# Banded attention: the mask of the maximum's scores moves from a matmul into VectorE's maximum

## The chip, the cores and the metric

The kernel runs on one NeuronCore of a Trainium2 chip. The metric is the time of one execution on the device, in microseconds (us), as the median of several runs. The chip's engines work side by side and wait for each other on semaphores: TensorE (PE in the profile; its weight loads are PEld), VectorE (DVE), ScalarE (ACT), GpSimd (POOL), and SyncE (SP), which here only issues transfers.

## The reference

A transformer of four layers on `x` of 2 x 1024 tokens with 128 channels: full attention, a mixture of experts, banded attention, a mixture of experts, each with a layer norm before it and a residual. What matters here is the banded attention, with 16 heads of width 8:

```python
scores = jnp.einsum('bhid,bhjd->bhij', q, k) * SCALE
valid = (j <= i) & (j >= i - W + 1)          # W = 32
scores = jnp.where(valid, scores, -jnp.inf)
attn = jax.nn.softmax(scores, axis=-1)
out = jnp.einsum('bhij,bhjd->bhid', attn, v)
```

So each query looks at itself and the 31 tokens before it; b and s come from the input, 2 and 1024.

## The kernel before

The banded attention (`attend_banded`) works on NG = 8 groups: 2 batches by 4 groups of 4 heads. A group has 1024 tokens, in 8 tiles of 128. The softmax needs two passes over the scores.

**First pass, for the maximum.** Queries lie on the partitions. For each query tile `qt`, `scores` on TensorE fills two PSUM banks `sc[0]` and `sc[1]`, one for each pair of heads, each 128 x 320: two heads h of BAND = 160 keys (128 of the tile and 32 before it). Each bank first gets a mask (0 inside the band, -1e30 outside) by a matmul of the identity with `mask_q` (L604, 320 columns); then the products of q and k are added onto it, one matmul per head (L609, 160 columns, 48 rows). `reduce_tile` on VectorE takes the negated maximum of each bank in one instruction for both heads (L716). The first tile of a group has no keys before it and uses a mask of its own, `mask_q0`, and 128 columns in L609. The two banks are all there is: the next tile's scores wait until VectorE has read them (`red_done`).

**Between the passes.** After a group's eighth tile, `cut_max` on VectorE splits the maxima into three bf16 parts (four small instructions, L725 to L731), `turn_max` on TensorE transposes them (L632), `copy_max` on ScalarE copies them to SBUF (L684), and `max_rows` on SyncE writes them in six transfers into rows 48 to 50 and 112 to 114 of the queries `qs` (L563).

**Second pass.** Keys lie on the partitions. For each key tile `s`, TensorE fills two banks `st` with a mask (L656) and the products of k with q and its rows of the maximum (L661), ScalarE takes the exponential (L697), and `weigh` on TensorE multiplies by the values (L624).

**Order.** A prologue computes all 8 score tiles of group 0 and the first 4 of group 1. Then stage n is the second pass of group n in 8 steps s; beside it go the score tiles of later groups: steps 0 to 3 hold tiles 4 to 7 of group n+1, steps 4 to 7 hold tiles 0 to 3 of group n+2. TensorE's order in one step is: L656 twice, L661 four times, then the score tile (L604 twice, L609 four times), then `weigh` of the step before. `turn_max(n+1)` stands at the end of step 4. Step 0 of a stage waits for the group's maximum rows (`max_ready`), and step 4 waits for the transfer of group n+2's q and k (`loaded`), since its scores begin there. Stage 6 holds only tiles 4 to 7 of group 7, stage 7 none. SyncE's queue holds, for each stage n, first the 12 transfers of group n+2 (`load_group`, L232; q and k, three sizes), released when the second pass of group n-1 has issued its last product, and then the six of `max_rows(n+1)`. The stages are written as a hardware loop of 2 turns with 3 stages each and two stages behind it.

## Time and profile before

| | us |
|---|---|
| time, median of 3 runs | 1291.75 (1291.39 to 1293.16) |
| the profiled execution's own time | 1291.06 |
| its span in the trace | 1289.2 |
| banded attention in the span, first score matmul to last `weigh` | 817.5 to 957 |
| VectorE busy in the span | 1031.3 (80%) |
| TensorE busy in the span | 1087.0 (84%) |

The span is the time from the first to the last instruction that the profile holds; the time holds 1.9 us more around it. "PE busy" counts a matmul from its start to its modelled end, so waits inside a queue of matmuls count in part as busy. The column PEclk is the clock that TensorE was granted, as a share of 2.4 GHz: 1.00 is 2.4 GHz, 0.50 is 1.2 GHz. In a timeline, a row is a run of like instructions on one engine: start, length, engine, line, what it writes and reads, how many, and in brackets how long the engine was idle before it and for what.

### The profile page before, as it was taken

How to read it: one execution, taken by the hardware profiler on the slowest of the kernel's cores; microseconds unless marked ns; L12 is line 12 of the kernel's file. 1: busy time of each engine (PE TensorE's matmuls, PEld its weight loads, DVE VectorE, ACT ScalarE, POOL GpSimd, SP SyncE). 2: the span in 40 equal slices, each digit the busy share in tenths (PEclk: the TensorE clock that was granted, in tenths of full speed). 3: DMA queues.
4: the chain of work that ended last, by engine and by line, in shares of the span. 5: the costliest groups of instructions: out<-in, count | busy, mean ns of one | idle time of the engine just before them, and what ended most of it. 6: DMA issues, size and time to landing. Idle time of an engine off the chain costs nothing. (4 is left out here: it accounts for less than half of the span.)

```text
span 1289.2 us, 21879 instructions
## 1 busy us (share of the span) xinstructions
PE 1087.0 (84%) x6296; PEld 437.9 (34%) x6296; DVE 1031.3 (80%) x1765; ACT 720.8 (56%) x1103; POOL 400.7 (31%) x316
## 2 busy tenths in 40 slices
PE   4599999899998462999999995598975499999997
PEld 2112222222221051344444443233344244444443
DVE  6798999899999778788888886455537788888886
ACT  3207777677778522566666666045543356666665
POOL 1000000000000302676777770000001267777675
PEclk9658999899999776999999998589986699999999
DMA  2800000000002810767776651312100177766663
GB/s 66 249 4 26 26 27 1 27 26 21 6 2 93 278 32 3 162 161 166 161 162 158 155 117 47 102 52 58 45 2 20 44 177 165 159 156 155 162 161 95
DMA packets 53388, 120.14 MB, mean 93 GB/s; under 512 B 10296, under 2 KB 36792, under 8 KB 45128
## 3 DMA queue, kind: packets, MB, share of 16 engines
q1 hardware_dynamic: 53320, 119.28, 37.2%
q8 instruction: 37, 0.61, 0.2%
q14 instruction: 31, 0.25, 0.1%
HBM read 103.94 MB, written 14.91 MB: 92 GB/s over the span
## 5 line engine op out<-in xcount | busy, mean ns | idle before, releaser
L476 DVE TENSOR_REDUCE Aatt_mx<-Aatt_sc 128x1 f32<-128x512 f32 x512 | 317.4, 683 | 25.5 <-PE Aatt_sc L352 25.0
L436 ACT ACTIVATE Aatt_prob<-Aatt_st 128x1024 f32<-128x1024 f32 x256 | 247.3, 1022 | 76.5 <-PE Aatt_st L361 75.0
L1392 POOL TENSOR_TENSOR M1ex_low<-M1ex_hid,M1ex_high 128x512 f16<-128x512 f32 x132 | 180.8, 1387 | 95.0 <-ACT M1ex_high L1324 92.1
L1392 POOL TENSOR_TENSOR M2ex_low<-M2ex_hid,M2ex_high 128x512 f16<-128x512 f32 x132 | 179.6, 1378 | 94.5 <-ACT M2ex_high L1324 93.2
L352 PE MATMUL Aatt_sc<-ks,qs 48*128 48x512 bf16 x512 | 176.9, 432 | 27.3 <-DVE Aatt_mx L476 5.8
L372 PE MATMUL Aatt_pv<-Aatt_prob,vg 128*32 128x512 f32 x1024 | 143.4, 633 | 0.8 <-ACT Aatt_prob L436 0.6
L1363 DVE TENSOR_TENSOR M1ex_hid<-M1ex_act_up,M1ex_cb 128x512 f32<-128x512 f32 x132 | 138.4, 1049 | 4.9 <-DMA M1ex_cb<-comb 4.9
L1363 DVE TENSOR_TENSOR M2ex_hid<-M2ex_act_up,M2ex_cb 128x512 f32<-128x512 f32 x132 | 139.0, 1053 | 4.0 <-DMA M2ex_cb<-comb 4.0
L1354 DVE SCALAR_TENSOR_TENSOR M1ex_act_up<-M1ex_up,unscale,M1ex_sil 128x512 f32<-128x512 f32 x132 | 98.4, 746 | 37.0 <-ACT M1ex_sil L1319 34.6
L1319 ACT ACTIVATE M1ex_sil<-M1ex_gate,unscale 128x512 f32<-128x512 f32 x132 | 90.7, 687 | 64.9 <-PE M1ex_gate L1272 61.1
L1354 DVE SCALAR_TENSOR_TENSOR M2ex_act_up<-M2ex_up,unscale,M2ex_sil 128x512 f32<-128x512 f32 x132 | 98.4, 746 | 35.4 <-ACT M2ex_sil L1319 31.2
L1319 ACT ACTIVATE M2ex_sil<-M2ex_gate,unscale 128x512 f32<-128x512 f32 x132 | 90.7, 687 | 61.7 <-PE M2ex_gate L1272 57.9
L352 PEld LDWEIGHTS Aatt_sc<-ks,qs 48*128 48x128 bf16 x512 | 38.4, 95 | 227.1 <-DVE Aatt_mx L476 208.6
L326 POOL COPY vg<-A_vn 128x256 f32 (+1 forms) x8 | 3.2, 402 | 353.3 <-PE Aatt_pv L372 311.9
L361 PE MATMUL Aatt_st<-qs,ks 51*128 51x512 bf16 x512 | 102.2, 400 | 6.2 <-ACT Aatt_prob L436 3.6
L716 DVE TENSOR_REDUCE Batt_m<-Batt_sc 128x2 f32<-128x320 f32 x128 | 57.0, 488 | 60.8 <-PE Batt_sc L609 60.6
L1324 ACT CAST M2ex_high<-M2ex_hid 128x512 f16<-128x512 f32 x132 | 80.9, 613 | 34.1 <-DVE M2ex_hid L1363 32.0
L1324 ACT CAST M1ex_high<-M1ex_hid 128x512 f16<-128x512 f32 x132 | 80.9, 613 | 33.6 <-DVE M1ex_hid L1363 33.0
L697 ACT ACTIVATE Batt_prob<-Batt_st 128x320 f32<-128x320 f32 x128 | 49.0, 435 | 55.5 <-PE Batt_st L661 55.4
L1270 PE MATMUL M1ex_gate<-M_xh,M_wt 128*128 128x512 f16 x132 | 50.7, 384 | 27.1 <-DVEq L1348 23.9
L1270 PE MATMUL M2ex_gate<-M_xh,M_wt 128*128 128x512 f16 x132 | 50.5, 383 | 26.3 <-DVEq L1348 23.9
L1282 PE MATMUL M1ex_acc<-M1ex_low,M_wt 128*128 128x512 f16 x132 | 50.3, 381 | 2.0 <-POOL M1ex_low L1392 2.0
(271 smaller groups left out, 1774.8 us busy)
## 6 DMA issues: line engine op xcount, KB each, us to landing
M1ex_cb<-comb SPq DMA_DIRECT2D x64, 512.0 KB, 6.5
M2ex_cb<-comb SPq DMA_DIRECT2D x64, 512.0 KB, 6.5
M_wt<-wsplit SPq DMA_DIRECT2D x66, 192.0 KB
wsplit<-split_cut SPq DMA_DIRECT2D x9, 704.0 KB, 7.0
split_raw<-in_wg_dram SPq DMA_DIRECT2D x6, 704.0 KB, 5.1
stack<-Aqkv_part SPq DMA_DIRECT2D x16, 192.0 KB, 3.2
qs<-stack SPq DMA_DIRECT2D x32, 96.0 KB
ks<-stack SPq DMA_DIRECT2D x32, 96.0 KB
```

Of the source, the lines that this page charges most:

```text
L352: pe.matmul(sc_bank(k, i)[:, :], qs[k][rows, jp, qt * P:(qt + 1) * P], ks[k][rows, jp, h * CH:(h + 1) * CH], start=True, stop=True).then_i ...
L361: mm = pe.matmul(st[jp][:, half, :], ks[k][rows, jp, kc * P:(kc + 1) * P], qs[k][rows, jp, qh * CH:(qh + 1) * CH], start=True, stop=True)
L372: mm = pe.matmul(pv[32 * j:32 * j + 32, :], vg[k][:, kc, j, :], prob[(2 * s + j % PAIR) % 4][:, j // PAIR, :], start=kc == 0, stop=kc == T ...
L436: act.activation(prob[e % 4][:, :, :].rearrange("p a c -> p (a c)"), st[pr][:, :, :].rearrange("p a c -> p (a c)"), ACT.Exp, scale=SCALE). ...
L476: dve.tensor_reduce(mx[k][:, m, part // 2:part // 2 + 1], sc_bank(k, i)[:, :], AX.X, ALU.max).then_inc(red_done, 1)
L716: dve.tensor_reduce(m1[k][:, 2 * pr:2 * pr + 2, qt], sc[pr][:, :].rearrange("p (h r) -> p h r", h=2), AX.X, ALU.max, negate=True).then_inc ...
L1270: pe.matmul(o, wt[k][:, a, :], env.xh[:, cs], start=True, stop=False)
L1319: act.activation(sil[i % 2][:, :], gate[i % 2][:, :], ACT.Silu, scale=env.unscale[:, 0:1]).then_inc(sil_ready, 1)
L1324: act.copy(high[i % 3][:, :], hid[i % 3][:, :]).then_inc(high_ready, 1)
L1354: dve.scalar_tensor_tensor(act_up[i % 3][:, :], up[i % 2][:, :], env.unscale[:, 1:2], sil[i % 2][:, :], ALU.mult, ALU.mult).then_inc(up_re ...
L1363: dve.tensor_tensor(hid[i % 3][:, :], act_up[i % 3][:, :], cb[k][:, c * CH:(c + 1) * CH], ALU.mult).then_inc(hid_ready, 1)
L1392: pool.tensor_tensor(low[i % 3][:, :], hid[i % 3][:, :], high[i % 3][:, :], ALU.subtract).then_inc(low_ready, 1)
```

## The change

The mask matmuls of the first pass go. TensorE writes the products alone, each with `start=True`; for each head VectorE then runs one `tensor_tensor_reduce`, which adds the mask from SBUF to the scores in PSUM, negates, writes the result back over the scores and gives the minimum into `m1`. That is four instructions of 160 (first tile 128) elements for a tile instead of two of 320. The third mask goes, with its five GpSimd instructions in the set-up. In the same edit the hardware loop of the banded stages is replaced by eight stages written out, so that no wait counts on a register.

```diff
-        LOOPED = 6
-        def stages(eng, stage):
-            with eng.Fori(0, LOOPED // 3) as i:
-                for k in range(3):
-                    stage(i, k, True, True)
-            stage(LOOPED // 3, 0, True, False)
-            stage(LOOPED // 3, 1, False, False)
+        def stages(stage):
+            for n in range(NG):
+                stage(n // 3, n % 3, n + 1 < NG, n + 2 < NG)
...
             def scores(n, k, qt):
-                mask = mask_q if qt else mask_q0
-                for pr in range(2):
-                    pe.wait_ge(red_done, n * 2 * STEPS + 2 * qt + pr + 1)
-                    pe.matmul(sc[pr][:, :], env.ident16[:, :], mask[:, :], start=True, stop=True)
                 first = 0 if qt else WIN
                 for h in range(2):
                     for pr in range(2):
+                        if h == 0:
+                            pe.wait_ge(red_done, n * 2 * STEPS + 2 * qt + pr + 1)
                         rows = slice(HALF * pr, HALF * pr + MAXROW)
                         mm = pe.matmul(sc[pr][:, h * BAND + first:(h + 1) * BAND], qs[k][rows, h, qt * P:(qt + 1) * P],
-                                       ks[k][rows, h, qt * P - WIN + first:(qt + 1) * P], start=False, stop=True,
-                                       skip_group_check=True)
+                                       ks[k][rows, h, qt * P - WIN + first:(qt + 1) * P], start=True, stop=True)
                         if h == 1:
                             mm.then_inc(sc_done, 1)
...
             def reduce_tile(n, k, qt):
+                first = 0 if qt else WIN
                 for pr in range(2):
                     dve.wait_ge(sc_done, n * 2 * STEPS + 2 * qt + pr + 1)
-                    dve.tensor_reduce(m1[k][:, 2 * pr:2 * pr + 2, qt], sc[pr][:, :].rearrange("p (h r) -> p h r", h=2),
-                                      AX.X, ALU.max, negate=True).then_inc(red_done, 1)
+                    for h in range(2):
+                        j = 2 * pr + h
+                        scores = sc[pr][:, h * BAND + first:(h + 1) * BAND]
+                        ins = dve.tensor_tensor_reduce(scores, scores, mask_q[:, first:BAND], -1.0, -BARRED, ALU.add, ALU.min,
+                                                       accum_out=m1[k][:, j, qt:qt + 1])
+                    ins.then_inc(red_done, 1)
```

## Rows read from the trace of the kernel before

**Rows 1.** Groups of instructions, 812 to 950 us: count, busy us, mean ns, idle before.

```profile
L716 DVE TENSOR_REDUCE Batt_m<-Batt_sc 128x2 f32<-128x320 f32 x128 | 57.0, 488 | 60.8 <-PE Batt_sc L609 60.6
```

**Rows 2.** Windows: length, busy of each engine, PEclk, DMA share, GB/s.

```profile
817.00:839.00 22.00, 13.82 (x69) 3.99 (x69) 10.54 (x26) 1.54 (x2) 0.80 (x2) 0.50 0.21 58
839.60:849.90 10.30, 10.30 (x75) 2.72 (x74) 4.17 (x10) 3.06 (x8) 0.00 (x0) 0.50 0.25 73
850.00:957.80 107.80, 96.70 (x1207) 38.22 (x1206) 47.89 (x125) 56.89 (x144) 2.41 (x6) 0.97 0.14 39
...
943.00:946.00 3.00, 0.93 (x7) 0.32 (x7) 0.00 (x0) 0.48 (x2) 0.00 (x0) 0.96 0.00 0
```

**Rows 3.** Timeline of the prologue, last tile of group 0, and its maximum.

```profile
830.72 0.45 PE L609 MATMUL Batt_sc<-ks,qs 48*128 48x160 bf16 x4
831.20 0.89 DVE L716 TENSOR_REDUCE Batt_m<-Batt_sc 128x2 f32<-128x320 f32 x2 [0.92 <-PE Batt_sc L609]
...
834.08 3.74 SPq L563 DMA_DIRECT2D qs<-Batt_mt  x6
```

**Rows 4.** Timeline of stage 3, steps 1 and 2.

```profile
889.90 0.31 PE L609 MATMUL Batt_sc<-ks,qs 48*128 48x160 bf16 x4
...
890.25 0.89 DVE L716 TENSOR_REDUCE Batt_m<-Batt_sc 128x2 f32<-128x320 f32 x2 [0.65 <-PE Batt_sc L609]
...
890.55 0.45 PE L656 MATMUL Batt_st<-mask,ident 128*128 128x320 bf16 x2
...
891.18 0.45 PE L604 MATMUL Batt_sc<-mask,ident 128*128 128x320 bf16 x2
...
891.55 0.31 PE L609 MATMUL Batt_sc<-ks,qs 48*128 48x160 bf16 x4
...
891.80 0.48 PE L624 MATMUL Batt_pv<-Batt_prob,vg 128*32 128x160 f32 x8
```

**Rows 5.** Timeline of TensorE: steps of stages 0, 1, 3 and 4, one transpose.

```profile
839.60 0.71 PE L656 MATMUL Batt_st<-mask,ident 128*128 128x320 bf16 x2
...
849.89 0.56 PE L656 MATMUL Batt_st<-mask,ident 128*128 128x320 bf16 x2
...
864.41 0.45 PE L656 MATMUL Batt_st<-mask,ident 128*128 128x320 bf16 x2 [0.18 <-DMA ks<-stack]
...
887.37 0.44 PE L656 MATMUL Batt_st<-mask,ident 128*128 128x320 bf16 x2 [1.19 <-DMA qs<-Batt_mt]
...
893.86 0.45 PE L656 MATMUL Batt_st<-mask,ident 128*128 128x320 bf16 x2
895.50 0.26 PE L632 MATMUL Batt_turn<-ident,Batt_mparts 128*96 128x128 bf16 x1
...
901.53 0.44 PE L656 MATMUL Batt_st<-mask,ident 128*128 128x320 bf16 x2 [0.70 <-DMA qs<-Batt_mt]
```

**Rows 6.** Timeline of SyncE's queue: issues of maximum rows (L563) and loads (L232).

```profile
852.71 3.68 SPq L563 DMA_DIRECT2D qs<-Batt_mt  x6
...
862.01 0.74 SPq L232 DMA_DIRECT2D ks<-stack  x2
...
896.56 3.68 SPq L563 DMA_DIRECT2D qs<-Batt_mt  x6
900.62 0.81 SPq L232 DMA_DIRECT2D qs<-stack  x2
...
905.22 0.74 SPq L232 DMA_DIRECT2D ks<-stack  x2
...
924.83 17.32 SPq L563 DMA_DIRECT2D qs<-Batt_mt  x12
```

**Rows 7.** Groups of VectorE instructions, whole span, as Rows 1.

```profile
L820 DVE TENSOR_TENSOR Bout_att<-Bout_ut,Bout_rden 128x128 f32<-128x128 f32 x16 | 4.7, 292 | 0.6
...
L210 DVE TENSOR_TENSOR B_vn<-Bqkv_pv,b_bv 128x512 f32<-128x512 f32 x4 | 2.7, 688 | 2.6 <-PE Bqkv_pv L155 2.6
...
L92 DVE BATCH_NORM_AGGREGATE Aqkvln_mv<-Aqkvln_stats 128x2 f32<-128x6 f32 x16 | 1.2, 152 | 0.0
```

More of the change, by code:

```diff
@@ L536, in attend_banded @@
         block = ctx.enter_context(nc.Block())
-        mask_q, mask_q0, mask_k = env.masks
-        LOOPED = 6
-        def stages(eng, stage):
-            with eng.Fori(0, LOOPED // 3) as i:
-                for k in range(3):
-                    stage(i, k, True, True)
-            stage(LOOPED // 3, 0, True, False)
-            stage(LOOPED // 3, 1, False, False)
+        mask_q, mask_k = env.masks
+        def stages(stage):
+            for n in range(NG):
+                stage(n // 3, n % 3, n + 1 < NG, n + 2 < NG)
         def score_blocks(s, k, nxt, nxt2):
@@ L577, in stage @@
                     max_rows(n + 1, (k + 1) % 3)
-            stages(sp, stage)
+            stages(stage)
         @block.gpsimd
@@ L594, in stage @@
                     copy_v(n + 1, (k + 1) % 3)
-            stages(pool, stage)
+            stages(stage)
         @block.tensor
@@ L672, in stage @@
                 weigh(n, k, STEPS - 1)
-            stages(pe, stage)
+            stages(stage)
         @block.scalar
@@ L705, in stage @@
                         copy_max(n + 1)
-            stages(act, stage)
+            stages(stage)
         @block.vector
@@ L745, in stage @@
                             cut_max(n + off, kk)
-            stages(dve, stage)
+            stages(stage)
 def project_out(nc, env, tag):
@@ L881, in _ @@
                                    pattern=[[-1, P]], channel_multiplier=1).then_inc(made, 1)
-            pool.wait_ge(made, 7)
+            pool.wait_ge(made, 6)
             def keep(m, base, step, multiplier):
@@ L888, in keep @@
                                    pattern=[[0, 2], [step, BAND]], channel_multiplier=multiplier).then_inc(made, 1)
-            mq, mq0, mk = env.masks
-            for m in (mq, mq0):
-                keep(m, -1, 1, -1)
+            mq, mk = env.masks
+            keep(mq, -1, 1, -1)
             keep(mk, 0, 1, -1)
+            pool.wait_ge(made, 8)
+            keep(mq, WIN, -1, 1)
+            keep(mk, WIN - 1, -1, 1)
             pool.wait_ge(made, 10)
-            for m in (mq, mq0):
-                keep(m, WIN, -1, 1)
-            keep(mk, WIN - 1, -1, 1)
-            pool.wait_ge(made, 13)
-            keep(mq0, -WIN, 1, 0)
-            pool.wait_ge(made, 14)
             for m in (env.fresh, env.fresh_groups):
                 pool.memset(m[:, :, :], 1.0).then_inc(made, 1)
-            pool.wait_ge(made, 16)
+            pool.wait_ge(made, 12)
             for m in (env.fresh, env.fresh_groups):
                 pool.memset(m[:, :, 0:1], 0.0).then_inc(made, 1)
-            pool.wait_ge(made, 18)
+            pool.wait_ge(made, 14)
 def attention(nc, env, a, tag, attend):
@@ L1419, in transformer @@
         env.ident16 = sb("ident16", [P, P], BF16)
-        env.masks = [sb(f"mask{i}", [P, 2 * BAND], BF16) for i in range(3)]
+        env.masks = [sb(f"mask{i}", [P, 2 * BAND], BF16) for i in range(2)]
         env.gate = sb("gate_w", [P, E], F32)
```

## The prediction

> **What bounds the kernel now.** I read the page first, then the stretch of the banded attention by windows, groups, timeline and waits, since everything that changes in the run is there (817.5 to 957 us of the span). The groups say who waits: VectorE's 128 reductions are busy for 57.0 us, and VectorE is idle for 60.8 us before them, for the score matmuls [rows 1]. The windows say that there are three regimes [rows 2]: the prologue, with TensorE at half clock (1.2 GHz) and busy for 63%; the first 10 us of stage 0, still at half clock but without a gap; and the rest, at 2.4 GHz for nearly all of it.
>
> *Prologue.* TensorE and VectorE take turns on two banks. A tile takes 0.92 + 0.89 = 1.81 us: VectorE reduces for 0.89 us and waits 0.92 us, of which 0.48 us lie between the first product's start and the reduction's, and 0.44 us before that, which is the hand-over and the second mask matmul [rows 3].
>
> *Stages.* From one step's score products to the next's are 891.55 - 889.90 = 1.65 us: second pass 0.63, score mask 0.37, score products 0.25, `weigh` the remaining 0.40 [rows 4]. That looks as if 0.37 us of each step could be had. The timeline of the stages says otherwise. A stage begins when the maximum rows have landed; TensorE was idle for 1.19 and 0.70 us before that [rows 5]. From the transpose at the end of step 4 to the next stage's start there are 901.53 - 895.50 = 6.03 us: 1.06 us to the first issue (896.56), 3.68 us of issuing, the landing, and the start 4.97 us after the first issue [rows 5, 6]. Steps 5 to 7 lie under this chain; a shorter step there only lengthens TensorE's wait. What counts is the way from a stage's start to its transpose, 895.50 - 887.37 = 8.13 us. Before its last step lies a second chain, on SyncE: loads begin 4.06 us after the first maximum issue, take 905.96 - 900.62 = 5.34 us to issue, and step 4 may not begin before they land. In stage 1, where step 4 did wait for them, it began at 864.41, 1.66 us after the last issue ended at 862.75 [rows 5, 6]. So step 4 can't begin sooner than 6.1 us after the stage's start (4.06 + 5.34 + 1.66 - 4.97), and it begins 893.86 - 887.37 = 6.49 us after it now [rows 5, 6]. The clean stage-to-stage time is 8.13 + 6.03 = 14.16 us; the mean over five stages, from first maximum issue to first maximum issue, is (924.83 - 852.71) / 5 = 14.42 us, with the other stages' waits for loads and slower issues in it [rows 6].
>
> **The change, part by part.** *TensorE* loses the two mask matmuls of each of 64 tiles: 0.37 us a step at 2.4 GHz [rows 4], and at half clock between 0.53 us (640 columns) and 0.74 us (twice 0.37); I take 0.64. A step is then 1.28 us of TensorE's own work. At half clock the first four steps take 849.89 - 839.60 = 10.3 us, the first without `weigh` (about 0.7): 2.75 us a step, 2.1 after the change [rows 5].
>
> *VectorE* gets four passes for two. Call D its time from a tile's first to its last. The new operation is not in the trace. A two-input pass over PSUM takes 292 ns for 128 elements and 688 ns for 512 [rows 7], so 1.03 ns an element and 160 ns fixed: 325 ns for 160. Passes without a wait overlap: two reductions of 488 ns end after 0.89, so the second starts 0.40 after the first, some 0.09 before its end [rows 1, 4], and sixteen small instructions of 152 ns are busy for 1.2 us together, 0.075 us each [rows 7]. So a pass costs 165 + 75 = 0.24 us, and the last one 0.325. Lower bound: D = 3 x 0.24 + 0.325 = 1.05 us. Upper bound: each pass in full, with a small instruction for the minimum, and no overlap: 4 x (0.325 + 0.075) = 1.60 us. With the overlap and the small instruction it is 4 x 0.075 more than the lower one, 1.35. I take the middle, 1.30, against 0.89 now. The first tile has 128 elements, 0.13 less.
>
> The Trainium skill (VectorE: DVE Perf Modes, "Two Vector instructions with no wait between them") says that an operation that also writes out its accumulator is two instructions, the main one and a read of the accumulator. No row here shows it. By it the sum goes with 1.35, about 1.6 us later than mine; the same page's "Rules for kernel authors" asks for fewer instructions, which speaks against the change.
>
> *The turn between the two.* TensorE can now run the first product of bank 0 while VectorE still reads bank 1. After VectorE's last pass there follow 0.05 us of hand-over and the second and third product. The first three took 0.35 us to the reduction's start at 2.4 GHz (889.90 to 890.25) and 0.48 us at half clock [rows 3, 4]. I take 0.34 and 0.44 us from the end of one tile's passes to the start of the next's, where 0.65 and 0.92 stand now. A tile in a stage then takes D + 0.34 = 1.64 us, more than TensorE's 1.28: VectorE becomes the bound, and the 0.37 us is eaten. In the prologue: D + 0.44 = 1.74 against 1.81.
>
> *The sum.*
> - Prologue, group 0: seven turns of 0.07 less, 0.13 for the short first tile and 0.6 because its products start without the masks, against 0.4 because the last tile's passes take 1.30 for 0.89: -0.8 us.
> - Start of stage 0: now 839.60, 5.52 us after the maximum's first issue at 834.08, behind group 1's four tiles [rows 3, 5]. The rows land about 5 us after the first issue: -0.3 us.
> - Stage 0 to the next maximum's issue, 852.71 - 839.60 = 13.1 us [rows 5, 6]: five masks less at half clock are -3.2, but the last step, which ran at full clock (the clock rose at 850, rows 2), comes before the rise: +1.0, so 10.9. VectorE's chain gives 11.3: second pass at half clock 1.26 and turn 0.44, three steps of 2.1, D, and 834.08 - 832.09 = 1.99 from the last reduction's end to the issue [rows 3]. I take -1.8.
> - Five stages: from a stage's start, VectorE's first pass comes at 0.63 + 0.34 = 0.97; three tiles of D + 0.34; D; `cut_max` and hand-over 1.99 - 1.06 = 0.93: 2.92 + 4 D = 8.12 against 8.13. With 6.03 behind it 14.15 us: no gain over a clean stage. Of the 5 x (14.42 - 14.15) = 1.35 us of irregular waits I take -0.9, because TensorE reaches step 4 earlier in its work and SyncE and ScalarE lose the loop's turn. That covers the written-out loop too: its ends cost little since they lie under the maximum's transfers, and the longer instruction stream I price at 0, with up to 1 us either way.
> - Stage 6 to the last maximum: +0.1. Stage 7 has no scores. The set-up loses five GpSimd instructions; SyncE's loads end it, so 0.
>
> Together -0.8 - 0.3 - 1.8 - 0.9 + 0.1 = -3.7 us. The profiled execution's own 1291.06 us (span 1289.2 and 1.9 around it) becomes 1287.3. The median of the runs is 0.7 above that execution, so 1288.0 us.
>
> **Rivals.** D stands on this path 8 + 1 + 5 x 4 + 4 = 33 times, so 0.1 us of D is 3.3 us.
> 1. *The new passes are cheap* (D = 1.05): the prologue and stages 0 and 6 gain 13 x 0.25 = 3.2 more; the five stages stop at the loads: 6.1 + 0.63 + 0.25 + 0.41 = 7.4 to the transpose, a stage of 13.4, so 5 x 0.75 = 3.8 more. 1288.0 - 7.0 = 1281.0. For it: two-input passes run at one element a cycle. Against it: something has to write the minimum out.
> 2. *The new passes are dear and VectorE holds the stages up* (D = 1.60): +9.9 on -3.7, so 1297.9 us. It decides from D = 1.41, where the sum is zero. For it: every instruction here has 160 ns of its own, and twice as many are issued on the chain that decides; the scores are also written back. Against it: the overlap seen between reductions.
> 3. *It cancels* (D between 1.33 and 1.49): within 2.6 us of 1291.8. For it: the two maskings cost nearly the same, and the second chain is untouched.
> 4. *The clock stays low.* The granted clock was 1.2 GHz while TensorE was 63% busy, rose after 10 us at 100%, and fell to 1.2 GHz at 946 after a window at 31% [rows 2]. After the change TensorE's own work is 1.28 of 1.64 us in a step, and the full-height mask matmuls are half as many. If it never rises, a stage is 1.7 + 3 x 2.1 + 1.3 + 0.93 = 10.2 us to the transpose and three steps and a `weigh` behind it, 7.0: 17.2 us, so 5 x 2.8 and about 2.4 in the last stages on the first -2.9, about 1305. For it: less activity. Against it: at half clock TensorE has 2.1 us of work against VectorE's 1.74, no gap, and it is idle at every stage's start already. The Trainium skill (TensorE: Matmul & The Clock Gate, "What's actually happening") says that activity is what releases the clock; the windows agree.
>
> **Chances.** Forecast, D from 1.15 to 1.33 (1283 to 1289): 0.36. Rival 1: 0.16. Rival 3: 0.20. Rival 2: 0.20. Rival 4: 0.08. From no change a measurement here can tell about 0.2%, 2.6 us. Faster: 0.36 + 0.16 = 0.52; within: 0.20; slower: 0.28. The range reaches from rival 1's end to past D = 1.60: 1281 to 1299 us; the forecast's own is 1283 to 1289.
>
> **What the profile after would show.** L604 gone; the new VectorE row at 320 to 400 ns, four of them in 1.05 to 1.60 us, gaps of 0.34 us between tiles in the stages; a tile of about 1.74 us in the prologue; stages 14.2 us apart, waiting for VectorE before the transpose; TensorE's idle time up; the clock at 1.00 from about 850. It is wrong if D is over 1.41, if the clock falls inside the stages, or if the maximum rows or loads land at other times.

## The result and the profile after

| | before | after |
|---|---|---|
| median of 4 runs, us | 1292.05 (1291.39 to 1293.16) | 1278.21 (1273.47 to 1282.75) |
| the profiled execution's own time | 1291.06 | 1279.5 |
| its span | 1289.2 | 1277.7 |
| banded attention in the span, first score matmul to last `weigh` | 817.48 to 956.91 = 139.43 | 820.42 to 949.77 = 129.35 |
| VectorE busy | 1031.3 | 1051.1 |
| TensorE busy | 1087.0 | 1064.8 |

The ratio is 0.9893, with a 95% interval from 0.9864 to 0.9922: faster by 1.1%. The forecast was 1288.0 with a range from 1281 to 1299, so the time is below the range. The direction was right, the size was not: 3.7 us forecast, 13.8 measured (the prediction's 3.7 starts from 1291.75, the median of three runs). The set-up lost four GpSimd instructions and not five: one fill of the third mask and three that cut it to the band. In the profiled executions 10.1 us of the difference of 11.5 in span lie in the banded attention. Of the kernel before, two runs further down, 1303.34 and 1381.65 us, had a lower granted clock over the whole run (0.889 and 0.789 for about 0.90) and are left out of the ratios.

The groups of instructions from 812 to 945 us of the kernel after, to be read beside [rows 1]:

```profile
L712 DVE CUSTOM_DVE_ANT_0 Batt_sc<-Batt_sc,mask 128x160 f32<-128x160 f32 x224 | 66.1, 357 | 26.7 <-PE Batt_sc L602 26.7
...
L712 DVE DVE_READ_ACCUMULATOR2_ANT Batt_m<- 128x1 f32 x256 | 36.2, 141 | 0.0
...
L712 DVE CUSTOM_DVE_ANT_0 Batt_sc<-Batt_sc,mask 128x128 f32<-128x128 f32 x32 | 8.3, 322 | 6.0 <-PE Batt_sc L602 6.0
```

Each new pass is two rows, the pass of 357 ns and a read of the accumulator of 141 ns. VectorE is now idle for 26.7 + 6.0 us before its passes, where it was idle for 60.8 us. How long a tile really takes is in the timeline of the prologue, one tile and the start of the next, to be read beside [rows 3]:

```profile
822.35 0.33 DVE L712 CUSTOM_DVE_ANT_0 Batt_sc<-Batt_sc,mask 128x160 f32<-128x160 f32 x1 [0.41 <-PE Batt_sc L602]
822.60 0.14 DVE L712 DVE_READ_ACCUMULATOR2_ANT Batt_m<- 128x1 f32 x1
822.60 0.36 DVE L712 CUSTOM_DVE_ANT_0 Batt_sc<-Batt_sc,mask 128x160 f32<-128x160 f32 x1
822.88 0.14 DVE L712 DVE_READ_ACCUMULATOR2_ANT Batt_m<- 128x1 f32 x1
822.88 0.36 DVE L712 CUSTOM_DVE_ANT_0 Batt_sc<-Batt_sc,mask 128x160 f32<-128x160 f32 x1
823.07 0.10 PEld L602 LDWEIGHTS Batt_sc<-ks,qs 48*128 48x128 bf16 x1 [0.96 <-DVE Batt_m L712]
...
823.44 0.14 DVE L712 DVE_READ_ACCUMULATOR2_ANT Batt_m<- 128x1 f32 x1
...
823.99 0.33 DVE L712 CUSTOM_DVE_ANT_0 Batt_sc<-Batt_sc,mask 128x160 f32<-128x160 f32 x1 [0.41 <-PE Batt_sc L602]
```

The read of one pass and the next pass start together, and passes start 0.25 us (behind the first) to 0.28 us apart. From the first start to the end of the last read it is 823.58 - 822.35 = 1.23 us: that is D, forecast 1.30. The turn to the next tile is 0.41 us, forecast 0.44. At 823.07 TensorE loads for bank 0 while VectorE is still in bank 1, as foreseen.

The timeline around a transpose of the stages, from the kernel after, and the starts of stages 3 and 4. They answer to [rows 5, 6]:

```profile
861.17 0.33 DVE L712 CUSTOM_DVE_ANT_0 Batt_sc<-Batt_sc,mask 128x160 f32<-128x160 f32 x1 [0.34 <-PE Batt_sc L602]
...
863.26 0.59 ACT L694 COPY B_u<-Batt_pv 128x512 f32<-128x512 f32 x1
...
863.35 0.26 PE L624 MATMUL Batt_turn<-ident,Batt_mparts 128*96 128x128 bf16 x1 [0.18 <-DVE Batt_mparts L728]
...
863.73 0.29 ACT L676 COPY Batt_mt<-Batt_turn 96x128 bf16<-96x128 bf16 x1
...
864.10 3.67 SPq L558 DMA_DIRECT2D qs<-Batt_mt  x6
...
868.97 0.45 PE L648 MATMUL Batt_st<-mask,ident 128*128 128x320 bf16 x2 [0.38 <-DMA qs<-Batt_mt]
...
882.35 0.45 PE L648 MATMUL Batt_st<-mask,ident 128*128 128x320 bf16 x2 [0.34 <-DMA qs<-Batt_mt]
...
891.05 4.44 SPq L558 DMA_DIRECT2D qs<-Batt_mt  x6
...
896.72 0.72 PE L648 MATMUL Batt_st<-mask,ident 128*128 128x320 bf16 x2 [1.35 <-DMA qs<-Batt_mt]
```

The transpose now waits for VectorE, 0.18 us, where it had no wait in stage 3 before. The turn is 0.34 us. From the transpose to the first maximum issue are 864.10 - 863.35 = 0.75 us, where it was 1.06; the copy of the maximum, L676, is ready to run almost as soon as the transpose ends. A clean stage is 882.35 - 868.97 = 13.38 us, forecast 14.15. The last three rows show one that is not clean: the maximum's issues took 4.44 us for 3.67, TensorE waited 1.35 us, and its first two mask matmuls then took 0.72 us for 0.45.

The windows of the kernel after show the clock behind the last of these (length, busy of each engine, PEclk, DMA share, GB/s), to be read beside [rows 2]:

```profile
820.50:840.00 19.50, 8.52 (x49) 2.63 (x48) 14.14 (x93) 1.54 (x2) 0.28 (x1) 0.50 0.19 52
840.50:850.00 9.50, 9.29 (x93) 3.65 (x93) 6.70 (x45) 3.86 (x11) 0.00 (x0) 0.56 0.31 84
850.00:949.00 99.00, 82.71 (x1076) 34.53 (x1074) 62.22 (x406) 54.23 (x140) 2.40 (x6) 0.95 0.16 43
...
893.00:896.00 3.00, 2.17 (x35) 0.82 (x34) 2.47 (x16) 1.67 (x5) 0.40 (x1) 1.00 0.05 10
896.00:899.00 3.00, 2.28 (x17) 1.00 (x17) 0.88 (x7) 0.79 (x3) 0.00 (x0) 0.59 0.58 169
899.00:902.00 3.00, 2.89 (x30) 1.05 (x29) 1.72 (x13) 1.10 (x4) 0.00 (x0) 0.50 0.41 97
```

TensorE's granted clock fell to 1.2 GHz at 896.6, at the end of the 1.35 us wait, and rose at 903.4. It fell once more, from 940.9 to 944.3, behind the 1.38 us wait before stage 7.

Why stage 4 began late shows in the traffic. Besides the kernel's own transfers, the queues carry the kernel's instructions in packets of 16 KB. The views show packets, MB and share for each queue: first the kernel after over the late passage (893 to 897), then over 879 to 930, and last the kernel before over 879 to 930.

```profile
q8 instruction: 1, 0.02, 2.0%
```

```profile
q8 instruction: 4, 0.07, 0.5%
```

```profile
q1 hardware_dynamic: 1776, 2.46, 17.3%
q14 instruction: 2, 0.02, 0.1%
```

The one packet of the late passage started at 893.85, while maximum rows were under way. The transfer issued at 893.50 landed 2.96 us later, where 1.74 is usual, and the issue behind it took 1.35 us for 0.59. The 14 traces kept here hold 98 passages from a stage's transpose to the next stage. From the first maximum issue to the last landing, 69 of them take 4.82 to 5.05 us and 29 take 5.16 to 6.43. In 28 of the 29 a 16 KB instruction packet starts in between, and in one of the 69. That the packet delays the transfers is read from this coincidence; no run moved a packet on purpose. Over the second turn of the hardware loop the kernel before has no such packet (none between 878.7 and 930.9; those of q14 are of 8 KB), the kernel after has four.

The 10.1 us, step by step, worked out from the timelines of both:

| stretch | before | after | gain | forecast |
|---|---|---|---|---|
| first score matmul to first transpose | 15.55 | 14.01 | 1.5 | 0.8 |
| that transpose to stage 0 | 6.57 | 5.99 | 0.6 | 0.3 |
| stage 0 | 18.07 | 15.15 | 2.9 | 1.8 |
| stages 1 to 5 | 72.04 | 69.69 | 2.4 | 0.9 |
| stage 6 | 15.08 | 13.53 | 1.6 | -0.1 |
| stage 7 | 12.12 | 10.98 | 1.1 | 0 |

The forecast's terms end at the maximum's issues and not at the stages' starts, so they stand beside the nearest stretch. In the table below "to transpose" is from a stage's start to its transpose, and "behind" from there to the next start.

| stage, after | 0 | 1 | 2 | 3 | 4 | 5 | 6 |
|---|---|---|---|---|---|---|---|
| to transpose | 9.32 | 7.78 | 7.78 | 7.77 | 9.17 | 7.77 | 7.78 |
| behind | 5.83 | 5.62 | 5.60 | 6.60 | 6.00 | 5.60 | 5.75 |

### The profile page after: what moved, and what is told of

The parts are those of the page before. It is cut to its first block and busy times, and to the rows that moved or that the text cites. A ratio compares the mean times of both kernels' runs of the same rounds, so it can differ in the third digit from the quotient of the medians.

```text
span 1277.7 us, 21430 instructions
## 1 busy us (share of the span) xinstructions
PE 1064.8 (83%) x6168; PEld 435.2 (34%) x6168; DVE 1051.1 (82%) x2149; ACT 719.0 (56%) x1102; POOL 401.5 (31%) x312
## 5 line engine op out<-in xcount | busy, mean ns | idle before, releaser
L712 DVE CUSTOM_DVE_ANT_0 Batt_sc<-Batt_sc,mask 128x160 f32<-128x160 f32 (+1 forms) x256 | 74.4, 353 | 32.8 <-PE Batt_sc L602 32.8
L602 PE MATMUL Batt_sc<-ks,qs 48*128 48x160 bf16 (+1 forms) x256 | 34.4, 259 | 21.9 <-DVE Batt_m L712 16.1
```

The lines of the kernel that those rows point to most:

```text
L712: ins = dve.tensor_tensor_reduce(scores, scores, mask_q[:, first:BAND], -1.0, -BARRED, ALU.add, ALU.min, accum_out=m1[k][:, j, qt:qt + 1])
```

## Experiments

Three sets of kernels were run, each set on one chip beside the kernel before. In the first set that kernel took 1293.60 us (median of 23 runs), in the second 1293.05 (11), in the third 1291.85 (7). Its runs were spread further than the four above: 1282.38 to 1303.34 in the first set. The ratios are to the kernel before of the same set, and differ a little from the quotient of the medians. The banded part is that of the one profiled execution of each kernel.

| kernel | median us | ratio (95%) | banded part |
|---|---|---|---|
| the kernel after again | 1278.65 | 0.9874 (0.9828 to 0.9921) | 129.56 |
| stages written out only | 1287.21 | 0.9961 (0.9929 to 0.9993) | 136.85 |
| mask in VectorE, loop kept | 1282.79 | 0.9915 (0.9883 to 0.9948) | 129.53 |
| no mask at all | 1277.47 | 0.9898 (0.9842 to 0.9953) | 129.97 |
| VectorE's half alone | 1298.26 | 1.0048 (1.0024 to 1.0073) | 150.72 |
| after, one more pass a tile | 1284.08 | 0.9924 (0.9906 to 0.9941) | 140.03 |
| written out, maximum's copy first | 1282.11 | 0.9911 (0.9877 to 0.9945) | 134.34 |
| after, bank by bank | 1277.40 | 0.9890 (0.9866 to 0.9915) | 130.01 |
| after, filler at stage starts | 1274.46 | 0.9857 (0.9814 to 0.9899) | 129.33 |
| bank by bank, both fillers | 1272.70 | 0.9856 (0.9816 to 0.9896) | 125.30 |
| bank by bank, filler in steps | 1277.75 | 0.9897 (0.9857 to 0.9938) | 130.02 |
| no mask, filler in steps | 1277.31 | 0.9874 (0.9817 to 0.9931) | 129.17 |

### The kernel after again, and the change in two parts

The kernel after was run once more, unchanged.

> The changed kernel again, as the others' neighbour on the same chip, and because its four runs spread over 9 us where the kernel before spreads over 2. Theory A with the clock: the time again 1274 to 1283, the low ones with TensorE's clock at 1.00 in all of stages 1 to 6, the high ones with a stretch at 0.50 in them, as from 896 to 904 us in the first profile. Rival: the spread was chance of four runs, all within 2 us now.

It took 1278.65 us, and its clean stages are again 7.78 and 5.60. It too has one slow passage behind stage 3's transpose (6.45) and then the clock at half from 893 to 900, stage 4 with 9.23 to the transpose. Both profiled executions of the kernel have it. The spread of the first four runs was not an accident of four: six more lie between 1273.91 and 1281.41. Whether the short ones keep the clock through all stages, as expected, is not shown, since the profiled execution was the longest.

The next kernel is the one before with the stages written out, and nothing else:

```diff
-        def stages(eng, stage):
-            with eng.Fori(0, LOOPED // 3) as i:
...
+        def stages(stage):
+            for n in range(NG):
+                stage(n // 3, n % 3, n + 1 < NG, n + 2 < NG)
```

> The kernel before with only the loop of the banded stages written out; masks stay on TensorE. Theory A (the gain is the mask's move: shorter way from a stage's start to the transpose, and a shorter prologue): between 0 and -1.5 us against 1292.0, stages still 14.1 to 14.2 us apart, 8.1 us from a stage's start to its transpose. Rival B (the written-out stages give a good part of the 13.8 us, by fewer register instructions, branches and table loads): -4 us or more.

Its median is 0.4% below that of the kernel before, about 5 us (0.9 to 9.2), where 0 to 1.5 had been expected: by the time alone the rival, 4 us or more, is not excluded. In the traces it has 2.6 us less in the banded part. Its clean stages are 8.13 to the transpose and 5.86 behind it, where before had 8.13 and 5.94 to 6.04: 0.08 to 0.18 us of each stage was the loop's. But stages 1 to 5 together take 72.06 us for 72.04, since two slow passages (6.68 and 6.74) took it back. The 2.6 us lie elsewhere: 0.3 in stage 0, 1.2 in stage 6, where the part behind fell from 7.06 to 5.86, and 1.15 in stage 7, from 12.12 to 10.97. In the kernel before a 16 KB instruction packet started at 942.69, under the last maximum transfer, which landed after 3.19 us for 1.75; TensorE waited 2.70 us, and the clock was low from 945.7 to 952.6. The written-out kernel waited 1.49 us and had it low from 948.0 to 951.4. So these 2.4 us are where a packet fell, and not clearly the loop's.

The other half: the mask in VectorE, with the hardware loop left on TensorE, ScalarE, GpSimd and SyncE, and VectorE alone written out. The loop on VectorE with the new passes was not tried.

```diff
-            stages(stage)
+            stages(stage, pe)      # on sp, pool and act in the same way
...
+            with eng.Fori(0, LOOPED // 3) as i:
+                for k in range(3):
+                    stage(i, k, True, True)
```

> The mask in VectorE as in the changed kernel, but with the loop kept on TensorE, ScalarE, GpSimd and SyncE (VectorE's part written out). Theory A: within 2 us of the changed kernel's 1278.2, so -11 to -14; stages 13.4 us apart, 7.8 us from start to transpose. Rival B: it loses 4 us or more of the gain, so 1282 or later.

Its banded part is 129.53 us, that of the kernel after. Clean stages are 7.78 and 5.70. So in the traces the mask's move carries the gain, and the written-out stages add at most 0.1 us a stage to it; the two parts do not add up. By the time it is less clear: the median, 1282.79, is 4.1 us above that of the kernel after in the same set and so on the side of the rival (1282 or later), but the two intervals overlap, and the profiled execution (1277.05) is one of its shorter ones.

### What VectorE's time does to the stages

VectorE's half of the change alone, on the kernel with the stages written out: TensorE still writes its masks, and VectorE adds the mask once more.

```diff
-                    dve.tensor_reduce(m1[k][:, 2 * pr:2 * pr + 2, qt], sc[pr][:, :].rearrange("p (h r) -> p h r", h=2),
-                                      AX.X, ALU.max, negate=True).then_inc(red_done, 1)
+                    for h in range(2):
...
+                        ins = dve.tensor_tensor_reduce(scores, scores, mask_q[:, first:BAND], -1.0, -BARRED, ALU.add, ALU.min,
+                                                       accum_out=m1[k][:, j, qt:qt + 1])
```

> VectorE's half alone: its four passes for a tile as in the changed kernel, but TensorE's mask matmuls stay (so the mask is added twice, which leaves the result as it is). Written-out stages. Theory A (a tile is VectorE's time D plus the turn to TensorE and back; both halves of the change act on this sum): D stays 1.23, the turn stays 0.65 us in the stages and 0.92 in the prologue; a prologue tile 2.15 us, start to transpose 1.34 + 3 x 1.88 + 1.23 + 0.93 = 9.1 us, stages 14.8 us apart, banded part about 5 us longer than the 136.9 of the run with only the stages written out. Rival (VectorE's extra time hides behind TensorE's): 136 to 138, start to transpose 8.1.

The timeline of its stage 3 shows two tiles:

```profile
909.62 0.33 DVE L715 CUSTOM_DVE_ANT_0 Batt_sc<-Batt_sc,mask 128x160 f32<-128x160 f32 x1 [0.65 <-PE Batt_sc L604]
...
910.72 0.14 DVE L715 DVE_READ_ACCUMULATOR2_ANT Batt_m<- 128x1 f32 x1
...
911.51 0.33 DVE L715 CUSTOM_DVE_ANT_0 Batt_sc<-Batt_sc,mask 128x160 f32<-128x160 f32 x1 [0.65 <-PE Batt_sc L604]
```

The turn is 0.65 us, as in [rows 4], and D is 910.86 - 909.62 = 1.24. A tile is 1.89 us, 0.24 more than the 1.65 of before, where TensorE still set the step. To the transpose there are three such tiles and the last D, which is 0.35 longer than 0.89: 8.13 + 3 x 0.24 + 0.35 = 9.20 us. Measured are 9.17 to 9.18 in five of seven stages. VectorE's passes set the transpose. The banded part missed its forecast, though: 13.9 us more than with the stages written out alone, where about 5 had been expected. The prologue took 2.6 us more, and stage 2 took 18.21 us with the clock low from 881 to 891.

Then the kernel after with one more pass a tile, a reduction of 160 elements of the mask that nobody reads:

```diff
                     dve.wait_ge(sc_done, n * 2 * STEPS + 2 * qt + pr + 1)
+                    if pr == 1:
+                        dve.tensor_reduce(extra[:, 0:1], mask_q[:, 0:BAND], AX.X, ALU.max)
```

> The changed kernel with one idle VectorE pass more in each tile (a reduction of 160 elements of the mask into a scratch column), which raises D by about 0.24 us. Theory A: D stands on the path about 33 times, so start to transpose 7.78 + 4 x 0.24 = 8.7 us, a prologue tile 1.89, the banded part 129.4 + 33 x 0.24 = 137 us. Rival (the loads or the maximum's transfers set the stages at 13.4, and VectorE only follows): start to transpose under 8.2, the banded part 129 to 132.

```profile
L711 DVE TENSOR_REDUCE Batt_extra<-mask 128x1 f32<-128x160 bf16 x58 | 18.2, 314 | 0.0
```

The groups from 830 to 950 show the pass with 314 ns. The transpose came after 8.85 us in stages 3, 5 and 6, 1.07 more than 7.78, so four tiles of 0.27. The banded part rose by 10.7 us, where the added passes make 33 x 0.27 = 8.9: besides them the clock was low at 865 to 871, 902 to 909, 919 to 923 and 940 to 953. The profiled execution, 1291.24 us, is the longest of the five, 7 us above their median.

Now the other way. This kernel leaves the first pass's mask out altogether, as its expectation says: two plain reductions of the raw scores a tile.

```diff
-                        ins = dve.tensor_tensor_reduce(scores, scores, mask_q[:, first:BAND], -1.0, -BARRED, ALU.add, ALU.min,
-                                                       accum_out=m1[k][:, j, qt:qt + 1])
...
+                    dve.tensor_reduce(m1[k][:, 2 * pr:2 * pr + 2, qt], sc[pr][:, :].rearrange("p (h r) -> p h r", h=2)[:, :, first:BAND],
+                                      AX.X, ALU.max, negate=True).then_inc(red_done, 1)
```

> Leaves work out: the maximum is taken over the unmasked scores, one reduction per bank, and no engine adds the mask there. It gives the price of the mask in VectorE. Theory A: VectorE's time for a tile falls from 1.23 to 0.89 us; the prologue's tile from 1.65 to about 1.30, so 3 us less with the start of stage 0; the stages can't fall under the 13.4 us which the loads of the group after next allow, so they gain 0 to 0.3 each: 1273 to 1275. Rival C (VectorE's chain still sets the stages): start to transpose 1.4 us shorter, stages 12.0 us apart, 1265. Rival D (the mask in VectorE is hidden): same as the changed kernel.

VectorE had its 0.89 us back and TensorE no masks to write, and the time was that of the kernel after, not the 1273 to 1275 us expected. The timeline from the first transpose that comes early, 6.68 us after its stage's start:

```profile
868.38 0.45 PE L648 MATMUL Batt_st<-mask,ident 128*128 128x320 bf16 x2 [0.54 <-DMA ks<-stack]
869.53 0.12 PEld L624 LDWEIGHTS Batt_turn<-ident,Batt_mparts 128*96 128x96 bf16 x1
...
869.82 0.59 ACT L694 COPY B_u<-Batt_pv 128x512 f32<-128x512 f32 x1
870.28 0.28 ACT L676 COPY Batt_mt<-Batt_turn 96x128 bf16<-96x128 bf16 x1
870.65 3.67 SPq L558 DMA_DIRECT2D qs<-Batt_mt  x6
...
874.44 1.85 SPq L232 DMA_DIRECT2D qs<-stack  x2
...
877.13 0.71 PE L648 MATMUL Batt_st<-mask,ident 128*128 128x320 bf16 x2 [3.04 <-DMA qs<-Batt_mt]
```

Step 4 waited 0.54 us for the loads: the second chain binds. The maximum's copy stands behind the 0.59 us copy of `B_u` again and the first issue is 1.12 us after the transpose. Then TensorE had nothing to do for 3.04 us, and the two mask matmuls behind that took 0.71 us. Of the 3.04 us, 1.6 are a late landing: an instruction packet started at 874.72, and the last maximum transfer, issued at 873.74, took 3.35 us. Before stages 1, 2, 4, 5 and 6 the wait was 0.9 to 2.0 us, where the kernel after has 0.34 to 0.75 in all stages but two. The windows of the same kernel:

```profile
875.00:878.00 3.00, 0.87 (x6) 0.36 (x8) 0.00 (x0) 0.00 (x0) 0.00 (x0) 0.66 0.29 102
878.00:881.00 3.00, 3.00 (x28) 1.09 (x24) 1.78 (x4) 1.53 (x4) 0.00 (x0) 0.50 0.60 159
881.00:884.00 3.00, 3.00 (x31) 1.32 (x34) 0.97 (x3) 1.06 (x3) 0.00 (x0) 0.50 0.01 3
```

The clock was at 1.2 GHz from 876.0 to 886.2, and the next stage needed 9.24 us to its transpose. What was won on VectorE's chain came back as waiting at a stage's end, and the low clock took it away.

### The copy of the maximum

Before with the stages written out, and ScalarE's copy of the turned maximum put ahead of its copy of `B_u`:

```diff
+                    if s == STEPS - AHEAD + TURN and nxt:
+                        copy_max(n + 1)
                     if s in (TB // 2, STEPS - 1):
...
-                    if s == STEPS - AHEAD + TURN and nxt:
-                        copy_max(n + 1)
```

> Masks on TensorE, stages written out, and ScalarE copies the turned maximum before it copies the first half of the output, where the kernel before has them the other way round. Theory S (part of the gain is that, with the transpose later than the last product, this copy no longer waits behind the other): from the transpose to the first issue 0.75 us for 1.06, transpose to next stage 5.55 instead of 5.86, so 7 x 0.3 = 2 us less in the banded part (136.9 to about 134.8). Rival: the copy's order costs nothing, 5.86 stays.

The timeline of ScalarE and SyncE, first in the kernel with the stages written out, then in this one:

```profile
883.00 0.26 PE L627 MATMUL Batt_turn<-ident,Batt_mparts 128*96 128x128 bf16 x1
883.14 0.58 ACT L697 COPY B_u<-Batt_pv 128x512 f32<-128x512 f32 x1 [0.23 <-PE Batt_pv L619]
883.62 0.27 ACT L679 COPY Batt_mt<-Batt_turn 96x128 bf16<-96x128 bf16 x1
...
883.98 3.67 SPq L558 DMA_DIRECT2D qs<-Batt_mt  x6
```

```profile
877.68 0.26 PE L627 MATMUL Batt_turn<-ident,Batt_mparts 128*96 128x128 bf16 x1
877.98 0.26 ACT L679 COPY Batt_mt<-Batt_turn 96x128 bf16<-96x128 bf16 x1 [0.38 <-PE Batt_turn L627]
878.14 0.58 ACT L699 COPY B_u<-Batt_pv 128x512 f32<-128x512 f32 x1
878.33 3.67 SPq L558 DMA_DIRECT2D qs<-Batt_mt  x6
```

The issue comes 0.65 us after the transpose and not 0.98; the part behind is 5.52 for 5.86 while the part to the transpose stays 8.13; and the banded part is 2.5 us shorter. The kernel after gets nearly the whole of this without the edit: there VectorE delays the transpose past the `weigh` that ends step 4, the copy of `B_u` starts before the transpose (863.26 against 863.35), and the copy of the maximum no longer waits for it.

### The order of the products, and the clock

The kernel after with the products of bank 0 first and then those of bank 1, so that the turn gets shorter:

```diff
-                for h in range(2):
-                    for pr in range(2):
+                for pr in range(2):
+                    for h in range(2):
```

> The changed kernel, but TensorE issues both products of bank 0 and then both of bank 1, so that bank 0 is full again while VectorE is still on bank 1. Theory A: the turn goes (0.34 us in the stages, 0.41 in the prologue): a prologue tile 1.2 to 1.3 us, start to transpose under 7.4 where the loads stop it, so 3 us less before stage 0 and 0.3 a stage, if the clock holds. Rival H (the clock falls, as without any mask, because TensorE does too little): stretches at 0.50 in half the stages, start to transpose 8 us and more there, no gain in the stages; banded part 127 to 130.

The prologue went from 14.01 to 11.00 us, and one stage ran at full clock with 7.01 and 5.74, 12.75 us. The other stages took 14.2 to 15.2, each with a stretch at low clock. The windows over its stage 3:

```profile
875.00:878.00 3.00, 2.52 (x29) 1.17 (x30) 2.05 (x15) 1.53 (x4) 0.00 (x0) 0.99 0.35 105
878.00:881.00 3.00, 3.00 (x28) 1.13 (x27) 1.54 (x11) 0.77 (x2) 0.00 (x0) 0.50 0.51 149
881.00:884.00 3.00, 2.83 (x38) 1.32 (x34) 2.55 (x17) 1.49 (x4) 0.00 (x0) 0.50 0.03 8
```

If the waits cost the clock and the clock the gain, then matmuls without use, put into the waits, should win it back. Four kernels put some there. All write a bank that the next real mask overwrites: "filler at starts" stands before a stage's wait for its maximum rows, "filler in steps" beside the second pass's mask. The first has four at each start:

```diff
+                if n:
+                    pe.wait_ge(exp_done, n * 2 * STEPS + 1)
+                    for _ in range(4):
+                        pe.matmul(st[k][:, :], env.ident16[:, :], mask_k[:, :], start=True, stop=True)
                 pe.wait_ge(max_ready, MAX_IN * n + MAX_IN)
```

> The changed kernel with four matmuls of the second pass's mask (320 columns each, into the bank that step 0 overwrites) before TensorE waits for a group's maximum rows, stages 1 to 7. They give nothing but work in the wait. Theory H (the clock falls in stage 3 or 4 because of the idle time before a stage, longest where the maximum's transfers are slow): no stretch at 0.50 between 850 and 935 us, stages 3 and 4 at 13.4 and 14.4 us for 14.4 and 15.2, banded part 129.5 to about 127.5. Rival (the stretch comes from the lower activity inside the steps): it stays, 129 to 130.

The banded part, 129.33, didn't move: a slow passage of 7.40 us behind stage 2's transpose still came before a low clock, at 881 to 884, and took about 1.8 us more than a clean one. What came back was 1.1 us in stage 7, 9.87 for 10.98, and 1.4 in stage 4, whose way to the transpose was 7.78 for 9.17.

The second has bank by bank, six at the starts and one more mask matmul in each step:

```diff
-                        pe.matmul(bank[:, :], env.ident16[:, :], mask_k[:, :], start=True, stop=True)
+                        for _ in range(2 - pr if n else 1):
+                            pe.matmul(bank[:, :], env.ident16[:, :], mask_k[:, :], start=True, stop=True)
```

> Products bank by bank, with six such matmuls before each stage's wait and one more in every step of stages 1 to 7 (TensorE's own work 1.41 us a step). Theory H: clock at 1.00 in stages 1 to 6, start to transpose 7.3 us, stages 12.9 to 13.2; with the prologue's 4 us less than the changed kernel's the banded part 121 to 124 us, the time 1270 to 1273. Rival (falls of the clock have another cause than TensorE's activity): as bank by bank alone, stages at 14 to 15 us and 130.

```profile
846.00:939.00 93.00, 85.49 (x1114) 40.84 (x1114) 57.22 (x376) 50.54 (x131) 2.00 (x5) 1.00 0.17 46
```

In its windows the clock is 1.00 from 846 to 939. The banded part is 125.30 us, a little over the 121 to 124 expected and the shortest of all, though the fillers lengthened the way to the transpose to 7.42, and though two passages behind a transpose were slow (6.92 and 7.07 us). At 1272.70 us (1271.71 to 1274.87) it has the lowest median here, but its ratio is that of the filler at stage starts, and its interval overlaps with most others. It differs from bank by bank alone, at 130.01, only in work that is of no use, and is 4.7 us shorter in the banded part, with one execution of each in the profile: that is what the held clock brought here, less the fillers' own time.

The third has bank by bank and two more mask matmuls a step, none at the starts:

```diff
+                        for _ in range(2 if n else 1):
+                            pe.matmul(bank[:, :], env.ident16[:, :], mask_k[:, :], start=True, stop=True)
```

> Products bank by bank, with two such matmuls more in every step of stages 1 to 7 and none in the waits: the mask matmuls' columns are those of the kernel before, but they stand in no exchange with VectorE (TensorE's own work about 1.55 us a step). Theory H: clock at 1.00, start to transpose 7.6 to 7.9, stages 13.3 to 13.6, banded part 124 to 126. Rival: 130 as without them.

Its banded part is 130.02, a miss: the way to the transpose was 7.83 to 7.88 where the clock was full, but the clock was low at 845 to 848 and 917 to 920, and two passages took 6.86 and 7.27. (The profiled execution, 1272.36 us, is the shortest of its four.)

The fourth leaves the first pass's mask out again and has two more mask matmuls of the second pass a step:

> Leaves work out: the maximum over unmasked scores, as in the run without any mask, with two such matmuls more in every step of stages 1 to 7. Theory H (that run was held back by the clock, in five of seven stages, not by the loads alone): start to transpose 7.4 to 7.6 instead of 8.5, stages 13.2 to 13.5 instead of 14.2 to 15.8, banded part 124 to 126 instead of 130. Rival (the run without the mask was bound by loads and transfers): about 130 again.

The banded part was 129.17, again a miss. One stage took 13.04 us, with 7.15 to the transpose; five others took 14.2 to 14.9, with the clock still low in three stretches and step 4 waiting up to 1.21 us for the loads.

## Why the prediction was wrong in size

**The bound, right.** The way from a stage's start to its transpose and from there over ScalarE, SyncE and the landing is what sets the stages, not TensorE's 1.65 us a step. [rows 5, 6] said so. The two kernels with more VectorE time moved with it; the one with less did so only in the one stage whose way was at full clock (6.68 us), where the loads bound it.

**D, mis-sized.** It is 1.23 and not 1.30. The prediction took the middle between an estimate with the accumulator's read (1.35) and a bound without it (1.05). There is a read, and it costs no time of its own on this chain but the last: it starts with the next pass. The Trainium skill (VectorE: DVE Perf Modes, "Two Vector instructions with no wait between them") says that such an operation is two instructions; the rows of 357 and 141 ns agree, and adding the second in full would have been wrong here. A pitch of 0.25 to 0.28 us carried the sum: 2.92 + 4 x 1.23 = 7.84 us to the transpose, measured 7.78, forecast 8.12. By the prediction's own count of 33 places this term is 33 x 0.07 = 2.3 us.

**"With 6.03 behind it", the step that failed.** The prediction took the part behind the transpose as unchanged. It is 5.60 us in clean stages. Of the 0.43, the kernels apart show 0.08 to 0.18 for the written-out stages, which were priced at nothing, and the rest for the copy of the maximum, which no longer stands behind the copy of `B_u` on ScalarE. The prediction had followed TensorE's and SyncE's queues past the transpose, but not ScalarE's, and the copy put first by hand shortened the banded part by 2.5 us, of which 7 x 0.34 us at most are the copy's own.

Both together make a clean stage 7.78 + 5.60 = 13.38 for 14.15, and five of them 3.9 us. Not all of it arrived: stages 1 to 5 gained 2.4 us. The slow passage before stage 4 cost 1.0 us, the low clock behind it 1.4 in stage 4's way to the transpose, and a second slow passage, behind that transpose at full clock, 0.4; on the other side 1.2 us of such irregular waits in the kernel before went. An instruction packet starts in each of the two slow passages, at 893.85 and 907.50. So the longer instruction stream, which the prediction priced at 0 with up to 1 us either way, is a second term of the prediction that the traces contradict: it brings packets into stages where the loop had none, and one of them, with the clock behind it, stands for 2.4 us.

**Stage 0 and prologue, mis-sized.** Tiles of the prologue are 1.65 us apart, forecast 1.74: seven turns make the 0.6 us that are missing, 0.5 of it D's. In stage 0 the first maximum issue came 850.69 - 840.42 = 10.27 us after the start, forecast 11.3. VectorE's first pass came at 1.39 and not 1.70; three steps took 847.56 - 841.81 = 5.75 and not 6.3, since the first interval holds no `weigh`, which the prediction had noted for TensorE's steps and not for VectorE's chain; and 1.90 followed D for 1.99.

**Stages 6 and 7.** 1.6 and 1.1 us came where nothing was forecast. The kernel with only the stages written out has nearly both (1.2 and 1.15). They are mostly not the change's: 1.3 us of them are the late landing of one transfer before stage 7 in the kernel before, under an instruction packet, and 1.1 the clock, which is low for 6.9 us of stage 7 before (945.7 to 952.6) and for 3.4 after (940.9 to 944.3). With one profile of the kernel before, it is not shown how often that happens to it.

**The remainder.** 13.8 us in the medians against 10.1 in the banded part. Of the profiled executions 1.4 us lie outside it. The stretch from the output projection to the second mixture takes 55 us in some executions and 58 to 60 in others, in kernels whose code there is the same: 55.2 after, 58.2 before, 60.0 with the stages written out alone. The two profiled executions of the kernel after alone have 55.2 and 60.0, so the edit does not set it. The interval of the ratio, 10.1 to 17.6 us, is for the whole time of one set of four runs each. The traces account for 10.1 us, 2.4 of them the packet and the clock of stages 6 and 7; what the rest of the 13.8 is, they don't show. Nor do the two mis-sized terms reach the measured time by themselves: 2.3 us for D and 5 x 0.43 = 2.2 for the part behind turn 1288.0 into 1283.5.

**The rivals.** Rivals 2 and 3 needed D above 1.33 and are out. Rival 1 had the right sign of the error and the wrong cause: D isn't 1.05 but 1.23, about a quarter of the way from 1.30, and its time came close by the copy and by irregular waits. Its floor was wrong as well: without any mask, step 4 waited for the loads at 868.38, 5.5 us after its stage's start (862.85), not 6.1; the loads began 3.8 us behind the first maximum issue for 4.06 and took 4.84 us to issue for 5.34. What it missed most is that a still cheaper VectorE brings nothing more: without any mask the banded part is 129.97 us. Rival 4 came true in part: the clock does rise, at 848.8, but it falls again in stages 4 and 7, which the prediction had named as a sign of being wrong, and costs 1.4 us in the first and 1.1 in the second (10.98 us, where two kernels with the same stage and the clock at 1.00 take 9.87) rather than 17. The Trainium skill (TensorE: Matmul & The Clock Gate, "What's actually happening") ties the clock to activity; the kernel with both fillers agrees, with 1.00 in place of 0.82 over 846 to 939 and 4.7 us less.

What sets the fall is more than the wait. The kernel with only the stages written out also waited 1.35 us, before its stage 5, and kept 1.00; so did bank by bank with filler in the steps after 1.42 us. Both have more mask matmuls in their steps than the kernel after, whose clock fell behind 1.35 us in both profiled executions. But bank by bank with filler in the steps also lost it, behind 1.02 and 1.84 us, and no mask with filler in the steps behind 1.25 to 1.51. So the runs show that more work on TensorE can hold the clock, and no rule for when it is enough.

**What stays open.** In nearly every kernel one or two passages behind a transpose are slow (5.9 to 7.6 us for 5.6), with maximum issues of 4.0 to 5.0 us for 3.67 or, where the last transfer is the late one, a landing of 2.7 to 3.4 us. Instruction packets start in 28 of the 29; that they are the cause no run separated, and the traces don't say which engine's instructions they hold. Nor is it settled why two more matmuls a step held the clock less well than one, with six at the starts: no run varied the one at a fixed number of the other.

## What to carry to other kernels

Behind a stage's bound, follow the result through every engine's queue down to the next stage's start: a copy of 0.59 us on an engine that was only half busy stood on the path in six of seven stages. Where the end of that path is a row of small transfers, look for instruction packets among them before pricing a longer program at nothing. Price an unseen pass by the pitch between its starts, not by the sum of its rows. And when a chain is shortened whose end is a fixed wait of TensorE, look at the granted clock behind that wait: past a point the next microsecond won there is paid back (no mask at all, 129.97 us), and cheap matmuls can then win more than the work saved (both fillers, 125.30).

## What the runs showed of the hardware that was not expected

- A `tensor_tensor_reduce` with an accumulator over 160 elements in PSUM is a row of 357 ns and one of 141 ns, at a pitch of 0.28 us (0.25 behind a tile's first); over 128 elements it is 0.25 us (0.21 behind the first).
- Around a wait of TensorE of 3.04 us the clock fell, and it was 0.50 for the next 6 us with TensorE busy throughout (3.00 of 3.00 us); after one of 0.34 us nothing happened; at one of 1.35 us, with 2.17 of 3 us busy ahead of it, it fell too in the kernel after, and in the kernel with only the stages written out one of 1.35 us left it at 1.00.
- The six transfers of maximum rows take 3.67 us to issue, and the last lands 1.7 us after its own issue began; in one or two stages of most kernels the same six take 4.0 to 5.0 us, or the last lands 2.7 to 3.4 us after its issue began.
- In 28 of the 29 slow passages a 16 KB packet of the instruction queue starts between the first issue and the last landing. Around the hardware loop's second turn no such packet comes for 52 us, in both kernels that keep the loop; written out, one comes every 9 to 15 us.
